# Sum and gate of the front batches' expert rows: from VectorE to GpSimd, in the tail of an adaLN and mixture-of-experts kernel

## The chip, the cores and the metric

One core of one Trainium2 chip runs the whole kernel. The time is device microseconds of one execution, as the median of several runs. "Before" is the kernel as it stood, "after" is the kernel with the change.

## The reference, cut to what matters

```python
mod = (silu(c) @ wmod).reshape(B, 6, 1, -1)          # B = 8 batches, S = 1024 tokens, D = 128
sa, ca, ga, sb, cb, gb = mod[:, 0] ... mod[:, 5]     # gb: the gate of the second half
x = x + ga * attention(layernorm(x) * (1 + ca) + sa)
h = layernorm(x) * (1 + cb) + sb
# ffn: 8 experts, the best 2 of each token, and a shared expert
sparse = sum over the 2 chosen experts e of w_e * (relu(h @ W1[e] + b1[e]) @ W2[e] + b2[e])
shared = relu(h @ Ws1 + bs1) @ Ws2 + bs2
out = x + gb * (sparse + shared)
```

What matters here is the last line. For each token two expert rows have to be added to each other, multiplied by the gate and added to the result.

## The kernel before, in words

Tokens lie 128 to a partition row: a batch is a tile of 128 partitions x 1024 float32 (8 tokens of 128 numbers in each partition). `res` holds the result of all 8 batches in SBUF. The kernel has three stages: attention (to about 300 us), the shared expert on batches 0 to 3 with routing tables (to about 340 us), and 47 expert tiles in a loop. At its end comes the tail, which is all that the change touches.

In the expert loop TensorE multiplies, VectorE evacuates and weights the rows, and GpSimd sends each row group to its token's place in `rows_z` in HBM by indirect DMAs (L780, the last ones L794). `rows_z` has two planes, one for each of a token's two experts.

In the tail, three things go on at once:
- TensorE computes the shared expert for batches 4 to 7, eight half batches i = 0 to 7 of 512 tokens. Its order is `last_up(i + 1)`, `last_down(i)`. `last_up(i)` needs VectorE's and ScalarE's split of the input (`last_x(i)`, on VectorE L1271). `last_down(i)` writes one of three PSUM banks and needs the evacuation of half batch i - 3 (`y_evac`).
- SyncE waits until all expert rows are sent (L460), then loads both planes of a batch into a slot of 128 x 2048 (`load_results`, L464, semaphore `z_loaded[b]`), in the order 4, 0, 5, 1, 6, 2, and batches 7 and 3 after the third store, since they reuse the first two slots. It stores each finished part (`store`, L471) when `fin_ready` has counted it, in a fixed order.
- VectorE works through an order written out by hand. "Front" batches are 0 to 3: their shared expert is already in `res`, so `add_front(b)` is three instructions on 128 x 1024 (L1652 adds the two planes, L1653 multiplies by the gate, L1654 adds to `res`). "Shared" half batches are `add_shared(i)`, four instructions on 128 x 512: L1640 adds the PSUM bank to the first plane, L1642 adds the second plane, L1643 multiplies by the gate, L1644 adds to `res`. `add_last_shared(7)` is L1672 to L1674, then L1676 on the PSUM bank and L1679.

VectorE's order from the arrival of batch 0's rows on:

```python
rows_into_result(0)
add_front(0)
last_x(5)
add_shared(1)
add_shared(2)
last_x(6)
add_front(1)
last_x(7)
add_shared(3)
add_shared(4)
add_front(2)
add_shared(5)
add_front(3)
add_shared(6)
add_last_shared(7)
```

Elsewhere, in attention, GpSimd has elementwise work of the same size: `add_shift` (L550: `res` plus a row broadcast over the tokens, in place), `scale_rows` (L564) and `shift_rows` (L571), and small ones in `rstd_2` (L554, L556).

Of the kernel before, what the change touches and what calls it, by code (L numbers as in the profile page):

```python
# [30 lines left out]
ALU = mybir.AluOpType  # L31
# [3 lines left out]
P = 128  # L35
B, S, D = 8, 1024, 128
G = S // P
# [23 lines left out]
FRONT = 8  # L61
# [49 lines left out]
def adaln_moe(nc, x, c_t, wmod, w_att, b_att, wg, packs, out):  # L111
    with ExitStack() as ctx:
        def sb(name, shape, dt=F32):
            return ctx.enter_context(nc.sbuf_tensor(name, shape, dt))
# [4 lines left out]
        def sem(name):  # L119
            return ctx.enter_context(nc.semaphore(name))  # L120
# [26 lines left out]
        mod = sb("mod", [P, B, 5, D])  # L147
# [200 lines left out]
        z_loaded = [sem(f"z_loaded{i}") for i in range(B)]  # L348
        fin_step = sem("fin_step")
        bias_step = sem("bias_step")  # L350
        fin_ready = sem("fin_ready")
        stored = sem("stored")

        x_v = x.rearrange("(b p g) d -> p b (g d)", b=B, p=P, g=G)
# [8 lines left out]
        z_slot = {b: z_at[i % len(z_at)] for i, b in enumerate(z_order)}  # L363
# [124 lines left out]
        def _(pool):  # L488
# [300 lines left out]
            for k in range(TILE // P):  # L789
                if k < TILE // P - 1:  # L790
                    pool.wait_ge(quarter_scaled, k + 1)
                else:
                    pool.wait_ge(y_ready, ROW_TILES)
                nc.gpsimd.indirect_dma_start(rows_z[:, :], bass.IndirectOffsetOnAxis(ap=tags[CYCLE - 2][:, k, 0:1].bitcast(I32), axis=0),  # L794
                                             tile_y[par][:, k, :], None, bounds_check=Z_ROWS - 1, oob_is_err=False).then_inc(y_sent[par], 16)


        @block.scalar
# [257 lines left out]
        def _(dve):  # L1056
# [535 lines left out]
            fin = Chain(dve, fin_step, 0)  # L1592
# [52 lines left out]

            def add_front(b):

                dve.wait_ge(z_loaded[b], 16)
                z0, z1 = (z_slot[b][:, k * S:(k + 1) * S].rearrange("p (g d) -> p g d", d=D) for k in range(2))
                gate = mod[:, b:b + 1, 4, :].to_broadcast([P, G, D])  # L1650
                r = res[:, b * G:b * G + G, :]
                fin(nc.vector.tensor_tensor(z0, z0, z1, ALU.add))  # L1652
                fin(nc.vector.tensor_tensor(z0, z0, gate, ALU.mult))  # L1653
                nc.vector.tensor_tensor(r, r, z0, ALU.add).then_inc(fin_ready, 1)  # L1654

            last = CYCLE - 4
# [27 lines left out]
            last_x(4)  # L1684
# [13 lines that stand above are left out]
# [379 lines left out]
```

## Time and profile before

| | before |
|---|---|
| median of 3 runs | 660.33 us |
| lowest, highest run | 659.73, 664.46 us |
| span of the profiled execution | 665.5 us |
| busy: TensorE, VectorE, ScalarE, GpSimd | 618.6, 457.9, 397.5, 343.3 us |
| mean granted TensorE clock | 0.982 of full |

The span is from the first to the last instruction of the one profiled execution. No time of its own is listed for that execution beside its span; the span is 5.2 us above the median of the runs. Busy times are sums over all stages, so they don't say which engine sets the end.

### The profile page before, as it was taken

How to read it: one execution, taken by the hardware profiler on the slowest of the kernel's cores; microseconds unless marked ns; L12 is line 12 of the kernel's file. 1: busy time of each engine (PE TensorE's matmuls, PEld its weight loads, DVE VectorE, ACT ScalarE, POOL GpSimd, SP SyncE). 2: the span in 40 equal slices, each digit the busy share in tenths (PEclk: the TensorE clock that was granted, in tenths of full speed). 3: DMA queues.
4: the chain of work that ended last, by engine and by line, in shares of the span. 5: the costliest groups of instructions: out<-in, count | busy, mean ns of one | idle time of the engine just before them, and what ended most of it. 6: DMA issues, size and time to landing. Idle time of an engine off the chain costs nothing.

```text
span 665.5 us, 13395 instructions
## 1 busy us (share of the span) xinstructions
PE 618.6 (93%) x4311; PEld 560.6 (84%) x4311; DVE 457.9 (69%) x1415; ACT 397.5 (60%) x635; POOL 343.3 (52%) x341
## 2 busy tenths in 40 slices
PE   3898999999999998977898999999999999999995
PEld 3587988898889886866798999998989898898995
DVE  7889797989898969766666564544444454452698
ACT  3587887877878756524346556565555646463541
POOL 4541706757575765657460465655565656465100
PEclk9899999999999999887999999999999999999998
DMA  8030000111111111111165466656666665521692
GB/s 299 27 158 1 1 1 17 37 34 33 34 33 38 33 42 33 37 39 43 49 196 200 129 197 190 181 172 193 195 188 182 187 182 178 175 65 30 268 386 113
DMA packets 29884, 76.44 MB, mean 115 GB/s; under 512 B 7126, under 2 KB 11374, under 8 KB 29712
## 3 DMA queue, kind: packets, MB, share of 16 engines
q1 hardware_dynamic: 20480, 58.49, 27.2%
q0 software_dynamic: 8640, 16.93, 7.5%
q8 instruction: 23, 0.38, 0.3%
q10 hardware_dynamic: 720, 0.47, 0.2%
q14 instruction: 21, 0.17, 0.1%
HBM read 53.53 MB, written 23.24 MB: 115 GB/s over the span
## 4 chain that ended last, share of the span: by engine, by line
PE 33%; DVE 8%; issue 5%; another core or an unknown queue 2%; DMA 2%; POOL 2%; ACT 1%; SPq 0%; POOLq 0%; ACTq 0%; DVEq 0%
PE value L1940 12%; PE score L1733 5%; PE misc L1940 5%; PE score L1731 5%; PE score L1732 4%; PE value L1991 2%; POOL rows_x L576 2%; DVE h_hi L1271 1%; DMA h_t<-rows_z 1%; ACT work L967 1%; DVE tile_y L1560 1%; PE misc L1772 1%; DVE tile_y L1552 0%; DMA lw<-rows_x 0%
## 5 line engine op out<-in xcount | busy, mean ns | idle before, releaser
L780 POOL DMA_INDIRECT rows_z<-tile_y,tags x138 | 142.5, 1032 | 118.8 <-issue 37.5
L1731 PE MATMUL score<-h_hi,h_lo 128*128 128x512 f32 (+1 forms) x252 | 94.9, 376 | 3.9 <-DVE rows_all L1177 3.8
L1759 PE MATMUL value<-w_ring,work 128*128 128x129 f32 x768 | 93.8, 279 | 1.6 <-ACT work L840 1.0
L1759 PEld LDWEIGHTS value<-w_ring,work 128*128 128x128 f32 x768 | 91.2, 194 | 4.1 <-issue 1.6
L967 ACT ACTIVATE work<-score,w_ring 128x512 f32<-128x512 f32 (+1 forms) x96 | 53.2, 616 | 61.7 <-PE score L1733 44.5
L1733 PE MATMUL score<-h_hi,h_lo 128*128 128x512 f32 (+1 forms) x252 | 89.4, 355 | 0.0
L1732 PE MATMUL score<-h_hi,h_lo 128*128 128x512 f32 (+1 forms) x252 | 88.9, 353 | 0.0
L576 POOL DMA_INDIRECT rows_x<-work,slot x64 | 64.5, 1008 | 45.5 <-issue 16.3
L838 ACT ACTIVATE work<-work 128x1024 f32<-128x1024 f32 x64 | 67.2, 1050 | 27.2 <-DVE work L1168 22.1
L1168 DVE TENSOR_TENSOR work<-score,lw 128x1024 f32<-128x1024 f32 x64 | 76.6, 1216 | 2.7 <-PE score L1733 1.2
L967 ACT ACTIVATE work<-score,w_shared 128x512 f32<-128x512 f32 x64 | 39.9, 685 | 57.9 <-PE score L1733 45.6
L967 ACT ACTIVATE work<-score,rows_all 128x256 f32<-128x256 f32 (+1 forms) x92 | 44.2, 548 | 43.6 <-PE score L1733 37.5
L840 ACT ACTIVATE work<-work 128x1024 f32<-128x1024 f32 x64 | 67.8, 1059 | 2.0
L1731 PE MATMUL score<-q_hi,h_lo 128*128 128x512 f32 x128 | 54.4, 425 | 5.2 <-DVE work L1168 4.6
L1731 PEld LDWEIGHTS score<-h_hi,h_lo 128*128 128x128 f32 x252 | 48.1, 191 | 10.3 <-DVE rows_all L1177 3.8
L1733 PEld LDWEIGHTS score<-h_hi,h_lo 128*128 128x128 f32 x252 | 47.7, 189 | 7.2 <-issue 0.5
L1732 PEld LDWEIGHTS score<-h_hi,h_lo 128*128 128x128 f32 x252 | 48.1, 191 | 5.1
L1733 PE MATMUL score<-q_hi,h_hi 128*128 128x512 f32 x128 | 51.1, 400 | 0.3 <-issue 0.3
L1940 PEld LDWEIGHTS value<-w_shared,work 128*128 128x128 f32 x416 | 50.0, 198 | 1.5 <-ACT work L967 0.9
L1732 PE MATMUL score<-q_lo,h_hi 128*128 128x512 f32 x128 | 50.8, 397 | 0.4 <-issue 0.3
L1940 PE MATMUL value<-w_shared,work 128*128 128x128 f32 x416 | 50.7, 282 | 0.4 <-ACT work L967 0.4
L1275 DVE TENSOR_TENSOR h_lo<-w_ring,h_lo 128x512 fp32r<-128x512 f32 x24 | 16.6, 692 | 44.3 <-ACT h_lo L960 24.1
(254 smaller groups left out, 1269.0 us busy)
## 6 DMA issues: line engine op xcount, KB each, us to landing
w_ring<-packs SPq DMA_DIRECT2D x24, 578.0 KB
rows_all<-packs SPq DMA_DIRECT2D x23, 578.0 KB
lw<-rows_x SPq DMA_DIRECT2D x24, 260.0 KB
res<-x SPq DMA_DIRECT2D x8, 512.0 KB, 6.3
h_t<-rows_z SPq DMA_DIRECT2D x3, 1024.0 KB, 11.0
mod<-mod_rows SPq DMA_DIRECT2D x1, 2560.0 KB, 10.1
rows_z<-tile_y,tags POOLq DMA_INDIRECT x142
rows_all<-rows_z SPq DMA_DIRECT2D x2, 1024.0 KB, 13.0
```

Of the source, the lines that this page charges most:

```text
L576: nc.gpsimd.indirect_dma_start(rows_x[:, :], bass.IndirectOffsetOnAxis(ap=slot[b % 2][:, k, g:g + 1], axis=0), (rows_1, rows_2)[k][b % 2][ ...
L780: nc.gpsimd.indirect_dma_start(rows_z[:, :], bass.IndirectOffsetOnAxis(ap=tags[pos][:, k, 0:1].bitcast(I32), axis=0), tile_y[par][:, k, :] ...
L838: nc.scalar.activation(prob[:, t % 4, :], prob[:, t % 4, :], ACT.Tanh).then_inc(tanh_done, 1)
L840: nc.scalar.activation(prob[:, t % 4, :], prob[:, t % 4, :], ACT.Exp).then_inc(exp_done, 1)
L967: ins = nc.scalar.activation(hidden[par][:, c, 0:rows], score[:, c, 0:rows], ACT.Relu, bias=w[:, B1_AT + c:B1_AT + c + 1])
L1168: nc.vector.tensor_tensor(prob[:, t % 4, :].rearrange("p (h n) -> p h n", h=2), score[:, 2 * (t % 2):2 * (t % 2) + 2, :], lw[:, at:at + S] ...
L1275: nc.vector.tensor_tensor(w1_lo[par], w[:, 0:F], w1_hi[par].bitcast(F32), ALU.subtract).then_inc(w_split, 1)
L1731: nc.tensor.matmul(out, a_lo, b_hi, start=True, stop=False)
L1732: nc.tensor.matmul(out, a_hi, b_lo, start=False, stop=False)
L1733: return nc.tensor.matmul(out, a_hi, b_hi, start=False, stop=True)
L1759: ins = nc.tensor.matmul(value[:, s // 3, c0:c0 + D + 1], prob[:, t % 4, s * P:(s + 1) * P], normal[b % 3][:, t, :], start=(t == 0 and s % ...
L1940: ins = nc.tensor.matmul(yacc[par][:, k * D:(k + 1) * D], hidden[part][:, c, k * P:(k + 1) * P], w[:, W2_AT + c * D:W2_AT + (c + 1) * D], ...
```

## The change

GpSimd gets new instructions after its last indirect DMA: for each of the batches 0 to 3 it waits for the batch's rows, adds the two planes in place, waits for itself, multiplies by the gate in place, and counts `front_scaled`. VectorE's `add_front(b)` waits for that count and keeps only its last instruction. VectorE's order and SyncE's order stay as they are.

```diff
+        front_step = sem("front_step")
+        front_scaled = sem("front_scaled")
...
+            front = Chain(pool, front_step, 0)
+
+            def scale_front(b):
+
+                pool.wait_ge(z_loaded[b], 16)
+                z0, z1 = (z_slot[b][:, k * S:(k + 1) * S].rearrange("p (g d) -> p g d", d=D) for k in range(2))
+                front(nc.gpsimd.tensor_tensor(z0, z0, z1, ALU.add))
+                nc.gpsimd.tensor_tensor(z0, z0, mod[:, b:b + 1, 4, :].to_broadcast([P, G, D]), ALU.mult).then_inc(front_scaled, 1)
+
+            for b in range(FRONT // 2):
+                scale_front(b)
...
             def add_front(b):
 
-                dve.wait_ge(z_loaded[b], 16)
-                z0, z1 = (z_slot[b][:, k * S:(k + 1) * S].rearrange("p (g d) -> p g d", d=D) for k in range(2))
-                gate = mod[:, b:b + 1, 4, :].to_broadcast([P, G, D])
+                dve.wait_ge(front_scaled, b + 1)
+                z0 = z_slot[b][:, 0:S].rearrange("p (g d) -> p g d", d=D)
                 r = res[:, b * G:b * G + G, :]
-                fin(nc.vector.tensor_tensor(z0, z0, z1, ALU.add))
-                fin(nc.vector.tensor_tensor(z0, z0, gate, ALU.mult))
                 nc.vector.tensor_tensor(r, r, z0, ALU.add).then_inc(fin_ready, 1)
```

## Rows read from the trace of the kernel before

**Rows 1.** The chain that ended last, its last stretch: start us, us, what.

```profile
620.39 6.03 DMA h_t<-rows_z
626.45 1.24 DVE h_t L1652
...
662.33 0.69 DVE res L1679
```

**Rows 2.** Busy time of each engine in stretches of the tail.

```profile
core 0: us, PE busy (x) PEld busy (x) DVE busy (x) ACT busy (x) POOL busy (x), PEclk, DMA share, GB/s
...
620.00:625.00 5.00, 5.00 (x38) 4.64 (x37) 2.06 (x3) 1.84 (x4) 0.00 (x0) 1.00 0.75 272
...
640.00:645.00 5.00, 5.00 (x34) 4.52 (x34) 4.86 (x8) 1.74 (x4) 0.00 (x0) 1.00 1.02 401
...
655.00:660.00 5.00, 3.19 (x29) 3.00 (x27) 4.86 (x7) 0.00 (x0) 0.00 (x0) 1.00 0.25 105
```

**Rows 3.** VectorE in order of time: start us, us, instruction.

```profile
628.97 1.23 DVE L1654 TENSOR_TENSOR res<-res,h_t 128x1024 f32<-128x1024 f32 x1
...
640.53 0.68 DVE L1271 TENSOR_TENSOR h_hi<-h_t,h_hi 128x512 fp32r<-128x512 f32 x1
641.13 0.68 DVE L1640 TENSOR_TENSOR work<-misc,work 128x512 f32<-128x512 f32 x1
641.85 0.69 DVE L1642 TENSOR_TENSOR work<-work 128x512 f32<-128x512 f32 x1
```

**Rows 4.** GpSimd in order of time, its elementwise work and its last instruction.

```profile
47.02 4.71 POOL L550 TENSOR_TENSOR res<-res,mod 128x1024 f32<-128x1024 f32 x2
...
104.14 2.38 POOL L564 TENSOR_TENSOR work<-rows_all,mod 128x1024 f32<-128x1024 f32 x1 [2.26 <-DVE rows_all L1155]
...
114.52 2.20 POOL L571 TENSOR_TENSOR work<-work,mod 128x1024 f32<-128x1024 f32 x1
...
617.64 0.98 POOL L794 DMA_INDIRECT rows_z<-tile_y,tags  x1 [0.30 <-issue]
```

**Rows 5.** DMA issues after 619 us: KB each, median us from issue to landing.

```profile
rows_all<-rows_z SPq DMA_DIRECT2D x2, 1024.0 KB, 13.0
...
w_ring<-rows_z SPq DMA_DIRECT2D x1, 1024.0 KB, 17.0
...
h_t<-rows_z SPq DMA_DIRECT2D x2, 1024.0 KB, 12.0
```

**Rows 6.** SyncE's queue in order of time: loads of batches 1, 6, then 2, then 7, 3.

```profile
621.92 1.03 SPq L464 DMA_DIRECT2D rows_all<-rows_z  x2
622.99 0.48 SPq L464 DMA_DIRECT2D w_ring<-rows_z  x1
...
633.97 1.03 SPq L464 DMA_DIRECT2D h_t<-rows_z  x2
```

**Rows 7.** VectorE in order of time beside GpSimd's instructions of [rows 4].

```profile
48.16 1.25 DVE L1075 SCALAR_TENSOR_TENSOR shift<-moments,rstd 128x8 f32<-128x8 f32 x1
49.34 1.21 DVE L1168 TENSOR_TENSOR work<-score,lw 128x1024 f32<-128x1024 f32 x1
50.47 1.30 DVE L1075 SCALAR_TENSOR_TENSOR shift<-moments,rstd 128x24 f32<-128x24 f32 x1
...
105.76 0.84 DVE L1247 TENSOR_TENSOR hot<-hot,place 128x64 f32<-128x64 f32 x1
106.53 0.21 DVE L1248 TENSOR_TENSOR hot<-hot,place 128x64 f32<-128x64 f32 x1
```

**Rows 8.** VectorE and GpSimd in order of time about 132 and 302 us.

```profile
132.16 0.66 DVE L1116 TENSOR_TENSOR h_lo<-tile_y,h_hi 128x512 fp32r<-128x512 f32 x1
...
132.33 0.58 POOL L554 TENSOR_SCALAR rstd<-moments 128x8 f32<-128x8 f32 x1 [0.26 <-issue]
...
302.33 0.24 POOL L554 TENSOR_SCALAR rstd<-moments 128x8 f32<-128x8 f32 x1 [0.95 <-DVE moments L1065]
```

**Rows 9.** TensorE in order of time: last_up(6) begins, last_down(7) is the last.

```profile
641.75 0.48 PE L1731 MATMUL score<-h_hi,h_lo 128*128 128x512 f32 x1
...
654.45 3.74 PE L1940 MATMUL value<-w_shared,work 128*128 128x128 f32 x32
```

**Rows 10.** Busy time and granted TensorE clock in stretches about an idle TensorE.

```profile
26.00:28.00 2.00, 1.73 (x5) 1.40 (x6) 2.00 (x5) 2.00 (x6) 1.83 (x3) 0.68 0.01 4
28.00:30.00 2.00, 2.00 (x6) 1.54 (x6) 1.97 (x17) 1.97 (x3) 1.84 (x3) 0.50 0.00 0
30.00:32.00 2.00, 2.00 (x16) 1.83 (x15) 2.00 (x3) 0.99 (x2) 1.83 (x3) 0.97 0.05 10
...
303.00:304.00 1.00, 0.67 (x3) 0.19 (x1) 0.00 (x0) 0.00 (x0) 1.00 (x1) 1.00 0.00 0
304.00:306.00 2.00, 0.00 (x0) 0.00 (x0) 1.64 (x7) 0.00 (x0) 1.50 (x3) 1.00 0.00 0
306.00:307.00 1.00, 0.32 (x2) 0.35 (x3) 0.53 (x3) 0.00 (x0) 0.94 (x1) 0.80 0.20 67
...
310.00:315.00 5.00, 5.00 (x25) 5.00 (x25) 4.16 (x25) 2.78 (x5) 3.78 (x5) 0.50 0.18 56
...
317.00:318.00 1.00, 1.00 (x12) 1.00 (x11) 0.26 (x1) 0.21 (x1) 0.69 (x2) 1.00 0.20 67
```

## The prediction, made before any run of the change

> **What bounds the kernel now.** The last stretch of the chain of waits comes first. It goes from the DMA of batch 0's rows, which lands at 626.42 (620.39 + 6.03), to VectorE's L1652 and stays on VectorE until 663.02 (662.33 + 0.69); the last store makes up the rest of the span [rows 1]. The stretches of busy time show why: from 640 to 645 VectorE is busy for 4.86 of 5 us, and GpSimd for none; from 620 to 625 VectorE has 2.06 us [rows 2]. So VectorE sets the end of the tail from 626.4 on, 36.6 us without a real gap, and its work there counts one for one. GpSimd ends its last instruction at 618.62 and is then free [rows 4]. TensorE is the next limit: it works without a pause until 658.19 (654.45 + 3.74) [rows 9], and VectorE's two last instructions after that, on the last bank, need 0.7 us each (the last is in [rows 1]). The end of VectorE could therefore not fall below 659.6, a gain of at most 3.4 us, or 0.5%, whatever is taken from it.
>
> **What the change removes.** In each `add_front` L1652 and L1653 go. The first starts at 626.45 [rows 1], and L1654 behind them at 628.97 [rows 3], so the pair costs 2.52 us; there are four pairs: **-10.1 us** of VectorE's 36.6.
>
> **What it adds on GpSimd.** Eight instructions on 128 x 1024. The multiply has the form of L550 (in place, times a row that is broadcast): two took 4.71 us, so 2.36 each. The trace has no plain sum of two full tensors; the nearest rows are L564 with 2.38 and L571 with 2.20 [rows 4]. I take 2.38 for all eight, with 2.20 as the lower end. One batch is two of them and 0.1 to 0.15 us for the waits between: 4.9 us. The waits on GpSimd delay nothing else, since nothing is queued behind them there.
>
> **The new wait.** `add_front(0)` stands before everything else in VectorE's order, and there is no slack: the rows land at 626.42, the product is ready at about 631.3. Behind the waiting L1654 are queued L1271 of `last_x(5)` and all later parts, and SyncE's second store with the loads of batches 7 and 3. Cost: **+4.9 us** of VectorE. For batches 1 and 2 the rows land about 13 and 17 us after issues at 621.9 and 623.0 [rows 5, 6], that is near 635 and at 640, some 10 us or more before VectorE will come to those parts, so these two waits end early. Batch 3's load is issued at about 634.5 now, after the third store [rows 6]; with that store some 6 us later it is issued at 640.5 and lands 12 us after that [rows 5], near 652; VectorE comes to `add_front(3)` after 660. No wait there either.
>
> **What the two engines do to each other.** This term decides the sign. While GpSimd does its first L550 (47.02 to 49.38), VectorE's L1075, a tiny instruction on 8 numbers per partition, lasts from 48.16 to 49.41; the next L1075 starts at 50.47 and ends at 51.77, and GpSimd's second L550 ends at 51.73. Between them L1168, with one input in PSUM and one in SBUF, runs its usual 1.21 us beside GpSimd's work [rows 4, 7]. Again: GpSimd's L564 ends at 106.52, and VectorE's L1247, with both inputs in SBUF, ends at 106.60 after 0.84 us, where its twin L1248 takes 0.21 [rows 4, 7]. It holds in the other direction too: GpSimd's L554 takes 0.58 us when it starts within VectorE's L1116 (both inputs in SBUF, ends at 132.82) and 0.24 when it doesn't [rows 8]. So a VectorE instruction with two SBUF inputs and an elementwise instruction of GpSimd don't overlap; whichever comes second stands still. In the tail nearly everything on VectorE is of that kind: L1271, L1642 (and L1643, L1644 like it), L1654, L1672 to L1674. Only L1640, once for each shared half batch, and L1676 read PSUM. L1640 holds VectorE's queue for 0.72 us less what the next overlaps; start to start with L1271 before it, 0.60 [rows 3].
>
> Two of the eight GpSimd instructions are already in the wait for batch 0's product. The other six start as their rows land, and find VectorE busy. Each takes 2.38 us in which VectorE's next two-input instruction stands: 6 x 2.38 = 14.3. In a walk through VectorE's order, in which a waiting instruction of either engine goes as soon as the other's ends, two of the six begin under an L1640 and hide 0.6 each: 14.3 - 1.2 = **+13.1 us**. Part of each start is hidden: L1247 ended 0.08 after GpSimd, though it needs 0.21 alone, so about 0.1 us of a blocked instruction is done beforehand. With some twelve changes of hand this gives back **-1.2 us**. What the trace doesn't show is whether a waiting GpSimd instruction gets in between two VectorE instructions that are chained. If it never does, it starts only under an L1640, all six hide 0.6, and the term is 14.3 - 3.6 = 10.7, to which a late product can add. If nothing is hidden beforehand, the -1.2 goes.
>
> The Trainium skill has this as a rule: "SBUF - State Buffer", section "Who interferes with whom", says that a VectorE instruction with two SBUF inputs contends with a GpSimd instruction that reads SBUF, and that the later one is fully blocked. It speaks against the change, and by the rows at 48, 105 and 132 us the trace agrees; by its wording the 128 x 512 instructions of the tail, for which the trace has no such pair, would be blocked as well, and by a rule of free overlap the term would be zero.
>
> **TensorE behind it.** VectorE's delay moves `last_x(6)` from 640.5 [rows 3] to about 647; TensorE now starts `last_up(6)` at 641.75 [rows 9], so it idles some 5 us. From that start to the end it needs 16.4 us (658.19 - 641.75), and would end near 664, some 4 to 5 us before VectorE needs its last bank. So this idleness costs nothing at the full clock. It can cost something at the lower one (below).
>
> **The sum.** -10.1 + 4.9 + 13.1 - 1.2 = **+6.7 us** at the end of VectorE; the last store follows as before. The span of 665.5 would become 672.2. The span lies 5.2 us over the median of the runs; the stretch that matters is the same instructions in each run, so I carry the difference over: 660.33 + 6.7 = **667.0 us**, 1.0% slower. The ends: +4.2 with six hidden starts; +7.9 with none done beforehand.
>
> **Rivals.**
> (a) The engines overlap freely in the tail, since the rows that speak against it are of small VectorE instructions. Then VectorE loses 10.1, waits 4.9 for the first product and later a little for TensorE's banks: half batch 6 is complete only at about 654.5, after which come L1640 to L1644, L1672 to L1674, L1676 and L1679, some 6.3 us, so 660.8; batch 3's product may add up to 1 us. VectorE ends 1.2 to 2.2 us earlier, 659 us (658 to 659.3). It decides if the tail's VectorE instructions keep their 0.69 and 1.23 us beside GpSimd. Against it: every one of the rows at 48, 50, 105 and 132 us. For it: nothing but the difference in size. Chance 0.10.
> (b) The block holds, and TensorE's clock makes it worse. TensorE idles for 2.7 us (the idle parts of the stretches from 303 to 307), and at the end of that the granted clock falls from 1.00 to 0.50, its lower level of 1.2 GHz; it is back at 2.4 GHz, 1.00, at 317 to 318, about 10 us later [rows 10]. An idleness of 5 us at 642 would do the same. At half clock for 10 us TensorE loses 5: half batch 6, complete near 660 otherwise, is complete at about 665, and from there VectorE needs 6.3 us: 671.1 against 663.0, +8.1, or 668.5 us (to 671 if more of it is slow). It decides when the loss is over about 3.5 us, the slack of half batch 6. Against it: the low clock at 27 us was over after some 4 us [rows 10], which would cost only 2. Chance 0.16.
> (c) The change doesn't act, as VectorE wouldn't need GpSimd's results in time or stands elsewhere: excluded for batch 0 by the missing slack, so no chance of its own.
>
> **How the numbers follow.** Forecast (block, TensorE hidden) 0.70, (a) 0.10, (b) 0.16; 0.04 is left for things not seen. The forecast's own range is +4.2 to +7.9, 664.5 to 668.3; the runs before scatter from 659.7 to 664.5, which can shift a median by 1 us or so. The range of 663.0 to 670.5 takes in the forecast and nearly all of (b), and leaves (a) out. A measurement of this kernel can tell about 1% (6.6 us) from no change, so "slower" begins at 666.9, in the middle of the forecast. Slower: half of 0.70, nearly all of (b), 0.50. Same: the other half, (a), the rest, 0.48. Faster would need 653.7, which TensorE's end excludes: 0.02.
>
> **What the changed profile would show.** The block: L1642 to L1644 and L1271 between 633 and 657 at 2 to 3 us instead of 0.69, each ending within 0.1 us of a GpSimd instruction's end; six such, or fewer if L1640 covers starts. If they stay at 0.69, (a) is right. The first L1654 starts at 631.3, with a wait for GpSimd of 4.9 us. GpSimd's eight instructions at 2.2 to 2.4 us; if some show 2.9, they waited for VectorE. TensorE shows an idle stretch of about 5 us before `last_up(6)`; a granted clock under 1.00 behind it, and `add_shared(6)` waiting for TensorE, speak for (b). VectorE's last instruction should end near 669.7 on the span's scale. The prediction fails low if VectorE's chained instructions keep GpSimd out until L1640, so that much of its work falls under PSUM reads, and fails high if TensorE's clock decides.

## The result, and the profile after

| | before | after |
|---|---|---|
| median | 660.03 us (4 runs) | 665.75 us (4 runs) |
| lowest, highest run | 659.73, 664.46 us | 664.26, 666.48 us |
| ratio after to before | | 1.0069, 95% interval 1.0044 to 1.0094 |
| span of the profiled execution | 665.5 us | 664.5 us |
| VectorE's end minus landing of batch 0's rows | 36.60 us | 43.29 us |

The kernel is slower by 0.4 to 0.9%, 4.5 us by the ratio and 5.7 by the medians. The two spans would say the opposite: in the profiled execution of before the whole tail started late, batch 0's rows landing at 626.42 [rows 1] against 618.73 after the change, and 5.1 of these 7.7 us are there already at SyncE's first load of expert weights (339.83 against 334.69), long before anything that was changed. In every other profiled execution of this case the time is 1.7 to 1.8 us over the span; by that the profiled execution of before took some 667.2 us (an estimate), 7 us more than the median of its runs. So the tails are compared from that landing on, and the traced pair is no sample of the timed one.

The chain of waits of the changed kernel, the pieces that answer to [rows 1]; columns are start, us, what:

```profile
612.68 6.05 DMA h_t<-rows_z
...
618.80 2.36 POOL h_t L805
...
621.23 2.42 POOL h_t L806
...
661.33 0.69 DVE res L1690
```

The rows land at 618.73 and VectorE ends at 662.02: 43.29 us, where [rows 1] give 663.02 - 626.42 = 36.60. GpSimd is now in the chain. The stretches of busy time that answer to [rows 2]:

```profile
core 0: us, PE busy (x) PEld busy (x) DVE busy (x) ACT busy (x) POOL busy (x), PEclk, DMA share, GB/s
...
625.00:630.00 5.00, 5.00 (x38) 4.64 (x37) 4.90 (x5) 1.84 (x4) 3.44 (x2) 1.00 1.02 394
...
635.00:640.00 5.00, 0.49 (x1) 0.50 (x2) 4.93 (x5) 0.00 (x0) 2.54 (x1) 0.89 0.98 368
640.00:645.00 5.00, 5.00 (x14) 3.86 (x13) 4.93 (x5) 1.27 (x2) 3.01 (x2) 0.50 0.46 185
```

VectorE looks as busy as before, but with five instructions in 5 us instead of eight. Busy time counts an instruction that stands still, and that is the trap in this view. Instruction by instruction, VectorE, to be read against [rows 3]:

```profile
623.67 1.23 DVE L1665 TENSOR_TENSOR res<-res,h_t 128x1024 f32<-128x1024 f32 x1 [5.52 <-POOL h_t L806]
...
626.14 0.69 DVE L1656 TENSOR_TENSOR h_t<-h_t 128x512 f32<-128x512 f32 x1
626.86 2.75 DVE L1657 TENSOR_TENSOR h_t<-h_t,mod 128x512 f32<-128x512 f32 x1
629.64 2.75 DVE L1658 TENSOR_TENSOR res<-res,h_t 128x512 f32<-128x512 f32 x1
632.32 0.68 DVE L1654 TENSOR_TENSOR work<-value,work 128x512 f32<-128x512 f32 x1
633.03 2.31 DVE L1656 TENSOR_TENSOR work<-work 128x512 f32<-128x512 f32 x1
635.37 2.71 DVE L1657 TENSOR_TENSOR work<-work,mod 128x512 f32<-128x512 f32 x1
638.12 0.69 DVE L1658 TENSOR_TENSOR res<-res,work 128x512 f32<-128x512 f32 x1
```

And GpSimd in the same stretch, to be read against [rows 4]:

```profile
626.48 2.58 POOL L805 TENSOR_TENSOR rows_all<-rows_all 128x1024 f32<-128x1024 f32 x1 [2.84 <-DMA rows_all<-rows_z]
629.14 2.71 POOL L806 TENSOR_TENSOR rows_all<-rows_all,mod 128x1024 f32<-128x1024 f32 x1
632.43 2.36 POOL L805 TENSOR_TENSOR w_ring<-w_ring 128x1024 f32<-128x1024 f32 x1 [0.58 <-DMA w_ring<-rows_z]
634.87 2.67 POOL L806 TENSOR_TENSOR w_ring<-w_ring,mod 128x1024 f32<-128x1024 f32 x1
```

Each GpSimd instruction has a VectorE instruction of 2.3 to 2.75 us beside it that takes 0.69 elsewhere. It goes by turns: GpSimd's L805 comes at 626.48 while L1656 is at work and waits for it (2.58 instead of 2.36), L1657 waits for L805, GpSimd's L806 waits for L1657 (2.71), L1658 waits for L806. L1654, which reads PSUM, takes its 0.68 beside GpSimd's L805 of 632.43.

### The profile page after: what moved, and what is told of

Read it like the earlier page. It is cut to its first block, busy times and chain, and to the rows that moved or that the text cites. A ratio compares the mean times of both kernels' runs of the same rounds, so it can differ in the third digit from the quotient of the medians.

```text
span 664.5 us, 13395 instructions
## 1 busy us (share of the span) xinstructions
PE 618.1 (93%) x4311; PEld 560.3 (84%) x4311; DVE 462.7 (70%) x1407; ACT 398.1 (60%) x635; POOL 369.5 (56%) x349
## 4 chain that ended last, share of the span: by engine, by line
PE 41%; DVE 7%; issue 2%; another core or an unknown queue 1%; DMA 1%; ACT 1%; POOL 1%; SPq 0%; ACTq 0%; DVEq 0%; POOLq 0%
PE value L1951 15%; PE misc L1951 6%; PE score L1744 6%; PE score L1742 5%; PE score L1743 5%; PE value L2002 2%; DMA h_t<-rows_z 1%; DVE work L1657 1%; DVE h_hi L1285 1%; PE misc L1783 1%; DVE h_t L1657 1%; DVE res L1665 0%; DVE work L1656 0%; ACT work L981 0%
## 5 line engine op out<-in xcount | busy, mean ns | idle before, releaser
L782 POOL DMA_INDIRECT rows_z<-tile_y,tags x138 | 144.1, 1044 | 114.9 <-issue 41.7
L1770 PEld LDWEIGHTS value<-w_ring,work 128*128 128x128 f32 x768 | 89.7, 192 | 5.2 <-ACT work L854 2.2
L578 POOL DMA_INDIRECT rows_x<-work,slot x64 | 66.8, 1044 | 40.3 <-issue 16.9
L1951 PE MATMUL value<-w_shared,work 128*128 128x128 f32 x416 | 52.1, 285 | 0.6 <-ACT work L981 0.4
## 6 DMA issues: line engine op xcount, KB each, us to landing
rows_all<-rows_z SPq DMA_DIRECT2D x2, 1024.0 KB, 13.1
```

Source lines behind the costliest of these rows:

```text
L578: nc.gpsimd.indirect_dma_start(rows_x[:, :], bass.IndirectOffsetOnAxis(ap=slot[b % 2][:, k, g:g + 1], axis=0), (rows_1, rows_2)[k][b % 2][ ...
L1770: ins = nc.tensor.matmul(value[:, s // 3, c0:c0 + D + 1], prob[:, t % 4, s * P:(s + 1) * P], normal[b % 3][:, t, :], start=(t == 0 and s % ...
L1951: ins = nc.tensor.matmul(yacc[par][:, k * D:(k + 1) * D], hidden[part][:, c, k * P:(k + 1) * P], w[:, W2_AT + c * D:W2_AT + (c + 1) * D], ...
```

## The experiments

The first four kernels ran on one chip, where the kernel before takes 668.76 us; e5 and e6 on a second, r1 and r2 on a third, e7 and e8 on a fourth; on these three it takes 651.2 to 651.5. Since medians of different chips can't be compared, the table gives each kernel's ratio to the kernel before on its own chip, and from its trace the stretch from SyncE's first load of rows to VectorE's end. The changed kernel itself was not run on the first of these chips; the traces of e3 and e4 are set against its trace above.

| kernel | ratio to before, 95% interval | stretch, us |
|---|---|---|
| before / after, the traces above | 1.0069 (1.0044 to 1.0094) | 43.07 / 49.78 |
| e1_scratch_sum | 1.0299 (1.0219 to 1.0379) | 58.38 |
| e2_scratch_write | 0.9978 (0.9940 to 1.0016) | 43.05 |
| e3_gate_in_psum | 1.0070 (1.0044 to 1.0096) | 47.26 |
| e4_front0_later | 1.0060 (1.0033 to 1.0086) | 48.13 |
| r1_before | 0.9992 (0.9980 to 1.0004) | 45.90 |
| r2_after | 1.0049 (1.0033 to 1.0064) | 48.65 |
| e5_sum_only | 1.0012 (1.0002 to 1.0023) | 47.32 |
| e6_batch3_only | 1.0017 (1.0004 to 1.0030) | 47.50 |
| e7_sum_by_dma | 0.9967 (0.9954 to 0.9979) | 44.14 |
| e8_sum_by_dma_2_3 | 0.9968 (0.9953 to 0.9982) | 44.10 |

The traces of e1 to e4 stand beside the first row, those below them beside r1_before (why there are two kinds is told with r1 and r2).

**e1_scratch_sum: is it the waiting, or GpSimd's presence?**

```diff
+            scratch = lw[:, 0:S].rearrange("p (g d) -> p g d", d=D)
+            def load_pool(b):
+                pool.wait_ge(z_loaded[b], 16)
+                for k in range(2):
+                    front(nc.gpsimd.tensor_tensor(scratch, scratch, mod[:, b:b + 1, 4, :].to_broadcast([P, G, D]), ALU.mult))
```

> The kernel before, with eight extra GpSimd multiplies of 128 x 1024 on a buffer that nobody reads, two behind the arrival of each front batch's rows; VectorE's work is untouched and nobody waits for GpSimd. Measured by the stretch from the landing of batch 0's rows to VectorE's end (before 36.6 us, after the change 43.3 us). Block: each of the eight costs VectorE some 2 us, as the six in the changed kernel did, so the stretch is 51 to 53.5 us and the kernel about 15 us slower than before. Rival, the loss comes only from waiting for GpSimd's products: 36.6 us, no change.

Measured from the landing: rows at 624.93, VectorE's end at 676.93, 52.0 us, +15.4. By the ratio the kernel is 2.2 to 3.8% slower, some 15 to 25 us, so the trace lies at the lower end; it is of the fastest of the four runs, and why two of the others took 8 and 11 us longer is open. Nobody waits for GpSimd here, so the loss is not in waiting for its products. VectorE's 128 x 1024 instructions stand in the same way:

```profile
624.96 1.23 DVE L1665 TENSOR_TENSOR h_t<-h_t 128x1024 f32<-128x1024 f32 x1 [0.43 <-DMA h_t<-rows_z]
626.22 3.27 DVE L1666 TENSOR_TENSOR h_t<-h_t,mod 128x1024 f32<-128x1024 f32 x1
629.52 3.31 DVE L1667 TENSOR_TENSOR res<-res,h_t 128x1024 f32<-128x1024 f32 x1
```

**e2_scratch_write: what in GpSimd's work blocks?**

```diff
-                for k in range(2):
-                    front(nc.gpsimd.tensor_tensor(scratch, scratch, mod[...], ALU.mult))
+                for k in range(4):
+                    front(nc.gpsimd.iota(scratch, pattern=[[1, G], [G, P]], base=0, channel_multiplier=-G, ...))
```

> As e1_scratch_sum, but instead of each multiply two iotas of 128 x 1024 on the same buffer (1.02 us each in the trace of before), sixteen in all: they write SBUF and read none. If only a GpSimd instruction that reads SBUF is in VectorE's way: stretch 36.6 us within 0.3, time unchanged. Rival, any GpSimd instruction on SBUF blocks: each holds VectorE about 0.75 us, 16 of them 12 us, stretch near 48 us.

Landing to end: 625.21 to 661.82, 36.6 us, and the time unchanged. GpSimd is about as long at work as in e1, and VectorE's instructions keep their lengths beside it. GpSimd, then VectorE:

```profile
625.29 4.29 POOL L805 IOTA lw<- 128x1024 f32 x4 [7.83 <-DMA h_t<-rows_z]
...
626.50 1.22 DVE L1667 TENSOR_TENSOR h_t<-h_t,mod 128x1024 f32<-128x1024 f32 x1
```

So GpSimd's writing of SBUF isn't in the way. That its reading is, follows if nothing else in which an iota differs from a multiply matters, which these runs don't separate. The Trainium skill, "SBUF - State Buffer", section "Who interferes with whom", makes this same distinction, between a GpSimd instruction that reads SBUF and one that only writes it; the run agrees with it, 0.0 us against 15.4.

**e3_gate_in_psum: what in VectorE's work is blocked?** The gates of batches 4 to 7 are copied once to a PSUM bank that is free by then, and the multiply reads them there.

```diff
+            fin(nc.vector.tensor_copy(gates, mod[:, B // 2:B, 4, :]))
...
-                gate = mod[:, b:b + 1, 4, :].to_broadcast([P, K, D])
+                gate = gates[:, b - B // 2:b - B // 2 + 1, :].to_broadcast([P, K, D])
```

> The changed kernel, with one edit: VectorE's multiply in each shared half batch reads the gate from PSUM (copied there once, before the rows land), so it has one SBUF input. Block by two SBUF inputs: each of the five or six GpSimd instructions hides another 0.7 us under such a multiply, stretch 39.3 to 41 us instead of 43.3. Rival, the engines slow each other wherever the operands lie: 43.3 us.

Landing to end: 626.53 to 667.46, 40.9 us, inside what the block by two SBUF inputs gives; 2.4 us less than in the changed kernel. The same multiply that stood for 2.7 us passes beside GpSimd (VectorE, L1658 is the multiply here):

```profile
638.01 2.17 DVE L1657 TENSOR_TENSOR work<-work 128x512 f32<-128x512 f32 x1
640.21 0.69 DVE L1658 TENSOR_TENSOR work<-work,value 128x512 f32<-128x512 f32 x1
640.94 2.05 DVE L1659 TENSOR_TENSOR res<-res,work 128x512 f32<-128x512 f32 x1
```

The timed ratio, 1.0070, doesn't tell it apart from the change; a gain of 0.36%, which the 2.4 us would be, is within the two intervals taken together. The verdict rests on the trace.

**e4_front0_later: is the first wait a cost of its own?**

```diff
-            add_front(0)
             last_x(5)
             add_shared(1)
+            add_front(0)
```

> The changed kernel, with add_front(0) behind last_x(5) and add_shared(1) in VectorE's order, and the stores' order to match. If the wait for the first product is a cost of its own, the 3.4 us of work put in front of it hide in it: stretch 39.9 us. If GpSimd's two instructions block that work anyway, only the part with one SBUF input and the change of hand is gained: 42.1 to 42.8 us.

Landing to end: 623.31 to 664.94, 41.6 us. That is 0.5 us under what the block gave and 1.7 over what free hiding gave: 1.7 us are gained of the 3.4 that stand in front of the wait now. The trace shows why not more:

```profile
624.61 1.68 DVE L1286 TENSOR_TENSOR h_hi<-h_t,h_hi 128x512 fp32r<-128x512 f32 x1 [1.71 <-ACT h_hi L972]
...
626.92 2.18 DVE L1657 TENSOR_TENSOR h_t<-h_t 128x512 f32<-128x512 f32 x1
```

The two moved instructions that have two SBUF inputs beside GpSimd's work take 1.68 and 2.18 us instead of 0.69, and VectorE idles 1.71 us for ScalarE's half of the split before them, 1.3 of it after the rows had landed. The expectation counted only the part that reads PSUM, and missed that an instruction loses less when it comes while GpSimd is near its end. As with e3, the ratio doesn't resolve it.

**e5_sum_only and e6_batch3_only: parts of the change.** In e5 GpSimd only adds the planes and VectorE multiplies; in e6 GpSimd does both for batch 3 alone.

```diff
-                front(nc.gpsimd.tensor_tensor(z0, z0, z1, ALU.add))
-                nc.gpsimd.tensor_tensor(z0, z0, mod[...], ALU.mult).then_inc(front_scaled, 1)
+                nc.gpsimd.tensor_tensor(z0, z0, z1, ALU.add).then_inc(front_scaled, 1)   # e5
...
-            for b in range(FRONT // 2):
-                scale_front(b)
+            scale_front(FRONT // 2 - 1)                                                  # e6
```

> Half of the change: GpSimd only adds the two planes (four instructions), VectorE multiplies by the gate and adds to the result. Block: VectorE loses four instructions of 1.26 us (-5.0), waits 2.4 us for the first sum and stands about 2 us for each of the other three, less 0.6 for one that starts under a PSUM read: stretch 36.6 - 5.0 + 2.4 + 5.5 = 39.5 us (39.0 to 40.2). Rival, without the block: 34.0 us.

> GpSimd sums and scales only batch 3, which VectorE needs last; there is no wait for a product. Block: -2.5 us of VectorE's work and two stands of 2.06 us: stretch 38.2 us (37.5 to 38.5), so slower than before although no product is late. Rival, the loss lay in the first wait: 34.1 us.

e6 is as the block has it: no product is late, VectorE saves 2.5 us and loses 2.04 and 2.08 in two instructions, and the stretch is 1.6 us over that of r1_before:

```profile
629.56 2.73 DVE L1656 TENSOR_TENSOR rows_all<-rows_all,mod 128x512 f32<-128x512 f32 x1
632.33 2.77 DVE L1657 TENSOR_TENSOR res<-res,rows_all 128x512 f32<-128x512 f32 x1
```

From the landing, e5 has 40.8 and e6 41.1 us. Both expected stretches (39.5 and 38.2) were missed, since the kernel before has 39.7 and not 36.6 us in r1_before. That trace is from another chip, with nearly the same median (651.22 and 651.44 us). e5 is 1.4 us over r1_before, where +2.9 was expected. Its wait for the first sum and its three stands, one of them here, are together longer than expected (2.3 and 6.3 us in place of 2.4 and 5.5):

```profile
620.80 2.90 DVE L1656 TENSOR_TENSOR res<-res,work 128x512 f32<-128x512 f32 x1
```

But they fill 2.1 us in which VectorE is idle in r1_before, and 2.3 + 6.3 - 5.0 - 2.1 is +1.5.

**r1_before and r2_after: the same two kernels on another chip.**

> The kernel before once more, for a second profile of its tail. The stretch from the landing of batch 0's rows to VectorE's end should be 36.6 us where VectorE finds no idle time in it, more by as much as it waits for TensorE's banks or inputs where the rows land earlier beside TensorE's work.

> The changed kernel once more, on the same chip as r1_before. If VectorE is without idle time in both, +6.7 us at its end; if r1_before shows VectorE waiting for TensorE for some time in the stretch, that much less, since the block fills that wait.

On this chip the change costs 2.8 us by the medians (651.22 to 654.04), and its trace's stretch is 2.75 us longer. Rows of VectorE in r1_before say where the rest is:

```profile
608.20 1.22 DVE L1652 TENSOR_TENSOR h_t<-h_t 128x1024 f32<-128x1024 f32 x1
...
621.29 1.22 DVE L1654 TENSOR_TENSOR res<-res,rows_all 128x1024 f32<-128x1024 f32 x1
624.48 0.69 DVE L1271 TENSOR_TENSOR h_hi<-h_t,h_hi 128x512 fp32r<-128x512 f32 x1 [1.97 <-ACT h_hi L957]
```

VectorE stands idle for 1.97 us before `last_x(7)`, which needs ScalarE, which needs `last_up(5)`, and for 0.1 us before `last_x(6)`. And it reaches batch 0 only at 608.20, with no wait for the rows, which are there 0.9 us before (their load, issued at 601.52, landed 5.8 us later, at 607.3). So the stretch from the landing is 646.98 - 607.3 = 39.7 us, where 36.6 and these three pieces give 39.6. In the trace of [rows 9] SyncE's first load came 21.8 us before `last_up(6)`, here 24.9, so here VectorE runs ahead of TensorE and waits for it. In r2_after that idle time is gone and the stands are there:

```profile
615.69 2.73 DVE L1657 TENSOR_TENSOR h_t<-h_t,mod 128x512 f32<-128x512 f32 x1
618.46 2.82 DVE L1658 TENSOR_TENSOR res<-res,h_t 128x512 f32<-128x512 f32 x1
```

The sum by r2_after's own rows: -10.1 removed, +5.3 to the first product, +10.6 in six stands (three of the six GpSimd instructions have a PSUM read of VectorE beside them), less the 1.97, 0.1 and 0.9 us, is +2.8 beside the 2.75 measured. Why the rows come earlier beside TensorE's work on this chip is open.

**e7_sum_by_dma and e8_sum_by_dma_2_3: take the work off VectorE without GpSimd reading SBUF.** SyncE loads only the first plane, and an accumulating DMA from GpSimd's queue adds the second plane to it.

```diff
+                if 1 <= b < FRONT // 2:                                        # e8: 2 <= b
+                    sp.dma_start(z_slot[b][:, 0:S], z_v[b][:, 0, :]).then_inc(z_loaded[b], 16)
+                    return
...
+            for b in range(1, FRONT // 2):                                     # e8: range(2, ...)
+                pool.wait_ge(z_loaded[b], 16)
+                nc.gpsimd.dma_start(z_slot[b][:, 0:S], z_v[b][:, 1, :], accum_op=ALU.add).then_inc(z_summed[b], 16)
...
-                fin(nc.vector.tensor_tensor(z0, z0, z1, ALU.add))
+                if b == 0:                                                     # e8: b < 2
+                    fin(nc.vector.tensor_tensor(z0, z0, z1, ALU.add))
```

> The kernel before, with the plane sum of front batches 1, 2 and 3 made by the load itself: SyncE loads only the first plane, and GpSimd's queue issues an accumulating DMA of the second plane onto it; VectorE keeps gate and result. GpSimd computes nothing on SBUF. If only GpSimd's reads of SBUF stand in VectorE's way, VectorE loses 3 x 1.26 = 3.8 us and is blocked by nothing; TensorE's end limits the gain to 3.4 us where VectorE never waits, and to about 3.2 us on a chip like that of r1_before: 0.4 to 0.5% faster than before. Rival, the accumulating DMAs land late (two transfers in a row, or slow ones): VectorE shows a wait at add_front(1) or add_front(3) and the gain is less or negative. Second rival, descriptor work on GpSimd stretches VectorE's instructions over 0.69 and 1.23 us.

> As e7_sum_by_dma, but only for batches 2 and 3; batch 1, whose accumulating DMA landed 4 us after VectorE came to it, is summed by VectorE again. VectorE loses 2 x 1.26 = 2.5 us and waits for no product: on a chip like that of r1_before its end comes 2.5 us earlier, within 0.5 us of TensorE's limit, and the ratio is 0.996; a little better than e7_sum_by_dma (1.6 us earlier in its profile). If the DMAs of batches 2 and 3 land late too, it shows as a wait in front of their multiply.

Both are faster than before by 0.3% (0.9967 and 0.9968, intervals below 1), and so faster than the change, whose ratios lie above 1 on both chips on which it ran. In e7 the DMA for batch 1 was late, as its first rival had it; no instruction of VectorE is stretched:

```profile
623.03 1.23 DVE L1662 TENSOR_TENSOR rows_all<-rows_all,mod 128x1024 f32<-128x1024 f32 x1 [3.97 <-DMA rows_all<-rows_z]
```

In e8 that wait is gone, and another bound shows, TensorE:

```profile
624.64 0.69 DVE L1279 TENSOR_TENSOR h_hi<-h_t,h_hi 128x512 fp32r<-128x512 f32 x1 [1.97 <-ACT h_hi L965]
...
639.10 0.69 DVE L1648 TENSOR_TENSOR h_t<-misc,h_t 128x512 f32<-128x512 f32 x1 [0.63 <-PE misc L1949]
```

VectorE waits 0.63 us for the bank of half batch 6, and has nine instructions, 6.24 us, behind it. So e8 gains 1.8 us in its stretch where 2.5 were expected: the limit is not TensorE's last bank but the one before, as the work behind that bank is longer. e7 gains 1.76 where 3.2 were expected. Its late DMA is not the main reason, since the same bank would have held it up without that. There the bank was complete at 639.03 (635.29 + 3.74), and VectorE came to it only 0.14 us later:

```profile
635.29 3.74 PE L1949 MATMUL misc<-w_shared,work 128*128 128x128 f32 x32
...
639.17 0.69 DVE L1648 TENSOR_TENSOR h_t<-misc,h_t 128x512 f32<-128x512 f32 x1
```

## Why the prediction was right

The step on which the sign hung was the block, and it held. Its terms against the first pair of traces:

- **Removed, -10.1:** the pairs L1652 and L1653 are gone; nothing else on VectorE changed its length unblocked (L1665 has 1.23, as L1654 in [rows 3]).
- **First wait, +4.9:** the rows land at 618.73, L1665 starts at 623.67, 4.94 us. GpSimd's plain sum, for which there was no row, took 2.36 us, the multiply 2.42; 2.38 had been taken. (L550, which the working calls a multiply, adds its broadcast row; the price held all the same.) VectorE waits for no other product, as forecast.
- **The other six, +13.1 - 1.2 = +11.9:** six VectorE instructions last 2.75, 2.75, 2.31, 2.71, 2.75 and 2.74 us; less 0.69 each that is 11.87. The total is right, its parts are not. Only one of the six had a PSUM read beside it, not two, and it saved 0.4 us, not 0.6: 0.8 less was hidden than the 1.2 of the working. And each of the other stands cost 2.05 us, where 2.38 less two changes of hand at 0.1 is 2.18: over six that is 0.8 less. The two errors cancel, which is luck.
- **The open question** of that step, whether a waiting GpSimd instruction gets in between two chained VectorE instructions, is answered: it does, within the 0.03 us between L1656's end and L1657 at 626.86.
- **The sum, +6.7:** 43.29 - 36.60 = 6.69 us in the traces. In the timed runs it is 4.5 (by the ratio) to 5.7, and 2.8 on another chip. This is the part that was mis-sized: the carrying of one tail over to all runs. "It counts one for one" holds only where VectorE has no idle time in the tail, and r1_before shows a tail in which some 3.0 us are free. That the first chip's runs mix such tails is argued from this, not shown. On the other chip the loss lies even below the forecast's own lower end of +4.2. The change came out at 0.7%, under the 1% from which the working counted "slower"; the working had given the two sides nearly even chances, so nothing in it foresaw which. That limit was also too coarse, as the interval, 1.0044 to 1.0094, tells 0.7% from no change.

Rival (a), free overlap, fell with every stretched instruction, and with e1. Rival (b), TensorE's clock, was half right. TensorE in the changed kernel:

```profile
639.51 0.77 PE L1742 MATMUL score<-h_hi,h_lo 128*128 128x512 f32 x1 [5.13 <-issue]
...
648.71 0.48 PE L1742 MATMUL score<-h_hi,h_lo 128*128 128x512 f32 x1
...
651.56 3.74 PE L1951 MATMUL misc<-w_shared,work 128*128 128x128 f32 x32
```

It idled 5.13 us for `last_x(6)`, and the granted clock was 0.50 (1.2 GHz) from 640 to 645 and 0.93 on the mean from 645 to 650. From the start of `last_up(6)` to that of `last_up(7)` TensorE took 9.20 us (639.51 to 648.71); in the kernel before it took 6.31, from 641.75 [rows 9] to this row:

```profile
648.06 0.48 PE L1731 MATMUL score<-h_hi,h_lo 128*128 128x512 f32 x1
```

So the low clock cost TensorE 2.9 us, near the lower of the rival's two prices, 2 and 5. The bank of half batch 6 was complete at 655.30, and VectorE came to it at 655.78: the cover was 0.5 us, not the 3.5 of the working, and the 2.9 us are most of the difference. By the same numbers 0.5 us more of it would have begun to delay VectorE. In r2_after the idle time was 1.61 us and the clock stayed at 1.00.

The idleness of 5 us itself was forecast from a wrong row. The L1271 at 640.53 [rows 3] is that of `last_x(7)`; `last_x(6)`, for which `last_up(6)` waits, is this one in the kernel before and this one in the changed kernel:

```profile
636.27 0.69 DVE L1271 TENSOR_TENSOR h_hi<-h_t,h_hi 128x512 fp32r<-128x512 f32 x1
...
638.73 0.68 DVE L1285 TENSOR_TENSOR h_hi<-h_t,h_hi 128x512 fp32r<-128x512 f32 x1
```

Counted from the landing it stands at 9.85 us before and at 20.00 after, so it moved by 10.2 us and not by the 6.5 of the working. The new place, about 647 on the scale of before, and so the idleness, came out right even so. (The idle time that rival (b) puts at 2.7 us is 3.01 by the stretches of [rows 10]: 0.33 + 2.00 + 0.68. It changes nothing there.)

One sign that was announced was wrong: the stretched instructions were to end within 0.1 us of GpSimd's. L1657 ends at 629.61 and L805 at 629.06, 0.55 us apart. The gap goes with the length of the instruction: 0.08 us for the L1247 of [rows 7] (0.21 alone), 0.55 here (0.69 alone), and in e1 L1666 of 128 x 1024 (1.22 alone) ends at 629.49, 1.09 us after the GpSimd instruction that ends at 628.40. Each ends 0.13 to 0.14 us less than its own length after the other lets go.

The limit of any gain was set a little too low: not 659.6, from TensorE's last bank, but 660.9, from the bank before, complete at 654.62 with 6.24 us of VectorE's work behind it, which the working had only in rival (a), at 660.8. e7 and e8 ran into it.

## What to carry to other kernels

Moving an elementwise instruction with SBUF inputs from VectorE to GpSimd was no parallel work here, where VectorE's own instructions have two SBUF inputs: each GpSimd instruction of 2.36 us gave VectorE 1.26 us and took about 2. Look in the trace for small instructions with two SBUF inputs that end when GpSimd's do, before costing such a move at nothing, and count instructions in a stretch, not only busy time. If work must leave VectorE, look for a way in which GpSimd reads no SBUF: an accumulating DMA did it here, for batches whose rows are there early enough. And look for the next limit before counting the gain: here it was one PSUM bank of TensorE, which left 1.8 of the 2.5 us taken off VectorE.

## What the runs showed of the hardware that was not expected

- Four iotas of 128 x 1024 on GpSimd took 4.29 us beside VectorE's two-input instructions and cost them nothing (1.22 us each).
- An instruction that stands loses less than the length of the one it waits for: about 2.05 of 2.36 us on VectorE, at 128 x 512 and (in e1) at 128 x 1024, and 0.2 to 0.4 us on GpSimd behind a VectorE instruction of 0.69.
- An accumulating DMA of 512 KB into SBUF landed 9.9 us after its issue while the stores and loads kept the DMA engines full, and 5.3 us later in the tail; its issue took 0.86 to 0.99 us of GpSimd, and no VectorE instruction was longer for it.
- The kernel before took 651 us on three chips and 669 on another; in the runs of the result, whose chip isn't named, it took 660.
